# First phase of a fused RWKV, expert, attention and ternary layer: projections as three fp32r products, one activation table, joined scans, and statistics split over two engines

## The chip, the cores and the metric

One core of a Trainium2 chip runs the whole program. The metric is the device time of one execution in microseconds (us). The engines are named as in the profile: PE is TensorE (matmul), DVE is VectorE, ACT is ScalarE, POOL is GpSimd and SP is SyncE, which here only starts transfers. Each engine works through its own list of instructions strictly in the order of the code; semaphores tie the lists together.

## The reference, cut to what matters

The input x is (8, 256, 256): B = 8 sequences of T = 256 tokens with C = 256 channels. Four blocks follow each other, each with a residual and a layer norm. The change touches the first, and the routing of the second.

```python
shifted = pad(x, one token)[:, :-1]
xk = x * mix_k + shifted * (1 - mix_k)        # the same for v and r
k, v, r = xk @ Wk.T, xv @ Wv.T, xr @ Wr.T
# per channel, along the tokens, w = -exp(decay), u = first:
#   mo = max(mx, k + u);  out = (e^(mx-mo) num + e^(k+u-mo) v) / (e^(mx-mo) den + e^(k+u-mo))
#   ms = max(mx + w, k);  num, den, mx = e^(mx+w-ms) num + e^(k-ms) v, e^(mx+w-ms) den + e^(k-ms), ms
x = layernorm(x + (sigmoid(r) * out) @ Wo.T)
logits = x @ gate_w.T                         # top 2 of 8 experts, softmax of the two
x = layernorm(x + sum over the 2 of weight * expert(x))
x = layernorm(x + linear_attention(x))
x = layernorm(x + ternary_ffn(x))
```

## The kernel before

The first phase goes by sequences b = 0 to 7, in slots s. In slot s four engines work on four sequences at once: the next one's projections (s + 1), the recurrence of s, the output and residual of s - 1, and the normalised x1, the logits and the choice of experts of s - 2. Every engine has a function `a_slot(s)` whose lines are the order of its work; nothing else schedules it. Arrays of the phase are cut out of one tile called `arena`, so most rows read `arena<-arena`. A [128, 512] array is two channel halves (k = 0, 1) of 256 tokens.

- PE: `project(b, j, ...)` for j = 0, 1, 2 (k, v, r): the mix of x and the shifted x is folded into the weights `wA`, so a projection is two output halves times four products of 128 x 128 by 128 x 256 in fp32. The moving operand is `xs[b % 2]`, 257 columns per half, read from column 1 (the token) or column 0 (the one before it). Then `turn_x1` (transposes of x1), `logits`, `output` (by Wo) and `rank`.
- DVE: `exponents(s)` (a max, two scans, three subtractions), `finish_y(s - 1)`, `states(s)` (eB * v and two pairs of scans), `choose(s - 2)`, `residual(s - 1)` with `bn_stats` and `bn_aggr`, `outputs(s)` (four elementwise operations), `positions(s - 2)`.
- POOL: `deviation` turns mean and variance into the scale and bias of the norm (L1570, L1572, L1575), `weights` makes the routing weights, `scatter` sends x1 to the experts' rows in DRAM by indirect DMA.

After slot 6 the first table of expert tiles is ready, and the expert tiles begin on PE while sequence 7 ends.

Of the kernel before, what the change touches and what calls it, by code (L numbers as in the profile page):

```python
# [5 lines left out]
P = 128  # L6
# [39 lines left out]
FULL_AT = 5  # L46
FIRST = -(-(2 * FULL_AT * T - E * (P - 1)) // P)
# [27 lines left out]
def build(nc, xT, x, vecs, rows, consts, mask, Wk, Wv, Wr, Wo, gate_w, w_gate, w_up, w_down,  # L75
          Wq3, Wk3, Wv3, Wo3, W1, W2, W3, out):
    ctx = ExitStack()
    with ctx:
# [57 lines left out]
        ix8 = sb("ix8", [P, NT, 8], U32)  # L136
# [43 lines left out]
        xT_hi = sb("xT_hi", [P, KC, T], F32R)  # L180
        xT_lo = sb("xT_lo", [P, KC, T], F32R)
        x3_hi = sb("x3_hi", [P, KC, T], F32R)
        x3_lo = sb("x3_lo", [P, KC, T], F32R)
        fh = sb("fh", [P, 2, 2, T], F32R)
        fl = sb("fl", [P, 2, 2, T], F32R)

# [16 lines left out]
        def then(*shape):  # L203
            return at(place[0], shape)

        wA = at(0, (3, 2 * KC, C))
        xs = [then(KC, 1 + T) for _ in range(2)]
# [61 lines left out]
        rank_ok, row_ok, pos_ok, tanh_ok, topw_ok, scat_ok, scat2_ok = map(
            sem, ("rank_ok", "row_ok", "pos_ok", "tanh_ok", "topw_ok", "scat_ok", "scat2_ok"))  # L270
# [49 lines left out]
        def _(sp):  # L320
# [13 lines left out]
            def later(b):  # L334
# [3 lines left out]
                if b == 4:  # L338
                    sp.wait_ge(in_dnz, 1)
# [27 lines left out]
            sp.wait_ge(rp_mm, B)  # L367
# [29 lines left out]
        def _(pe):  # L397
# [15 lines left out]
            def project(b, j, dst, done):  # L413
                if j == 0:
                    pe.wait_ge(in_xsb[b % 2], 16 * (b // 2 + 1))
                if b == 0:
                    pe.wait_ge(cleared, 1)
                    pe.wait_ge(wcur_ok, j + 1)
                    pe.wait_ge(wprev_ok, j + 1)
                s = xs[b % 2]  # L420
# [1294 lines left out]
```

## Time and profile before

| | |
|---|---|
| median of 3 runs | 407.81 us (407.49 to 408.16) |
| the profiled execution, own time | 410.51 us |
| its span | 408.6 us |
| PE busy | 373.9 us, 92% |
| DVE busy | 293.4 us, 72% |
| ACT busy | 208.7 us, 51% |
| POOL busy | 129.6 us, 32% |
| first subtraction for eB, sequence 0 / sequence 7 | at 12.01 / 107.23 us |

The program's own time is a little above the span, which leaves out what lies around the first and last instruction. A row of the timeline gives start, length, engine, line, operation and operands; `x2` means two of them merged. Operations of one engine overlap a little, so what an operation costs its engine is the distance from its start to the next start (its pitch), while what waits for it waits for its end.

### The profile page before, as it was taken

The page shows a single profiled execution, that of the slowest core. Times are in us where ns is not written, and L with a number is a line of the kernel's source. Part 1 is how long each engine was busy: PE and PEld are TensorE (multiplying, and loading weights), DVE is VectorE, ACT ScalarE, POOL GpSimd, SP SyncE. Part 2 cuts the span into 40 slices and gives each one's busy share as a digit, 9 for nine tenths or more (in the row PEclk, how much of TensorE's full clock was granted, in tenths as well). Part 3 has the DMA queues.
Part 4 walks back from the last instruction along what each step waited for, and adds up shares of the span by engine and source line. Part 5 has one row for each costly group of instructions (what it writes and reads, how often), then busy time and mean ns, then how long its engine had stood idle before and what let it go on. Part 6 is the DMA issues. An engine that isn't in the chain of part 4 may idle for free.

```text
span 408.6 us, 7333 instructions
## 1 busy us (share of the span) xinstructions
PE 373.9 (92%) x2234; PEld 325.4 (80%) x2234; DVE 293.4 (72%) x774; ACT 208.7 (51%) x435; POOL 129.6 (32%) x226
## 2 busy tenths in 40 slices
PE   8999999999858999999999858999999999999781
PEld 8888888888747776777777656898999899999680
DVE  4978999999975455797453265686969687886642
ACT  5474577557745333455335322556555645645451
POOL 2002355544645500002301077435344340401111
PEclk9999999999979999999999987999999999999987
DMA  7842864301133456533431132102020200000000
GB/s 219 279 173 86 121 219 136 104 33 53 52 90 118 134 178 199 163 107 100 131 116 52 53 91 65 53 1 77 2 79 2 77 29 2 26 2 26 2 26 26
DMA packets 28565, 35.75 MB, mean 87 GB/s; under 512 B 3696, under 2 KB 25712, under 8 KB 28272
## 3 DMA queue, kind: packets, MB, share of 16 engines
q1 hardware_dynamic: 19696, 21.78, 18.0%
q0 software_dynamic: 3072, 8.39, 6.3%
q10 hardware_dynamic: 5760, 5.12, 3.6%
q8 instruction: 19, 0.31, 0.4%
q14 instruction: 18, 0.15, 0.1%
HBM read 22.83 MB, written 12.45 MB: 86 GB/s over the span
## 4 chain that ended last, share of the span: by engine, by line
PE 47%; DVE 28%; ACT 8%; issue 7%; POOL 7%; DMA 1%; SPq 0%; ACTq 0%; POOLq 0%; DVEq 0%
PE bank L400 18%; PE bank L547 10%; PE bank L568 8%; DVE st L1047 4%; POOL arena L1638 3%; POOL nm L1575 2%; PE bank L527 2%; PE bank L557 2%; PE bank L736 2%; DVE arena L1107 2%; PE bank L410 2%; DVE arena L1110 2%; POOL rs L1572 2%; DVE arena L1481 2%; ACT arena L798 1%
## 5 line engine op out<-in xcount | busy, mean ns | idle before, releaser
L400 PE MATMUL bank<-arena 128*128 128x256 f32 (+2 forms) x576 | 116.6, 357 | 1.7 <-issue 0.7
L400 PEld LDWEIGHTS bank<-arena 128*128 128x128 f32 x576 | 99.8, 190 | 14.8 <-DVE arena L1463 2.0
L798 ACT ACTIVATE arena<-bank 128x256 f32<-128x256 f32 (+1 forms) x118 | 45.5, 422 | 45.7 <-PE bank L568 30.1
L547 PE MATMUL bank<-gu,arena 128*128 x156 | 53.9, 469 | 0.0
L1570 POOL TENSOR_TENSOR ve<-mv,eps 128x2 f32<-128x2 f32 x32 | 6.8, 213 | 145.4 <-DVE mv L1051 143.6
L803 ACT ACTIVATE arena<-arena,nm,rs 128x256 f32<-128x256 f32 x48 | 26.2, 596 | 38.5 <-POOL nm L1575 38.4
L568 PE MATMUL bank<-dn,arena 96*128 x156 | 41.1, 386 | 4.6 <-DVE arena L1261 3.8
L1638 POOL DMA_INDIRECT arena<-yg,ypos x32 | 31.3, 977 | 38.9 <-DMA yg<-arena 30.5
L1261 DVE COPY arena<-bank 96x256 f32<-96x256 f32 x39 | 16.3, 419 | 36.1 <-PE bank L557 32.6
L568 PEld LDWEIGHTS bank<-dn,arena 96*128 96x128 f32 x156 | 28.6, 190 | 14.8 <-issue 6.9
L1610 POOL DMA_INDIRECT xg<-x,pos x32 | 34.3, 1073 | 14.6 <-issue 7.3
L547 PEld LDWEIGHTS bank<-gu,arena 128*128 128x128 f32 x156 | 27.1, 194 | 8.5 <-issue 0.5
L964 ACT ACTIVATE arena<-bank 128x512 f32<-128x512 f32 (+2 forms) x32 | 15.6, 488 | 25.0 <-PE bank L400 21.4
L887 ACT ACTIVATE arena<-bank 128x176 f32<-128x176 f32 x39 | 12.3, 315 | 30.8 <-PE bank L547 30.0
L400 PE MATMUL bank<-x_hi,w1q 128*128 128x256 f32 x96 | 26.5, 307 | 1.5 <-ACT x_hi L798 1.5
L1445 DVE SCALAR_TENSOR_TENSOR arena<-arena,bank 128x512 f32<-128x512 f32 (+2 forms) x32 | 17.8, 556 | 12.5 <-ACT arena L964 12.0
L681 PE MATMUL bank<-w3q,fh 128*128 128x256 f32 x96 | 24.2, 305 | 1.4 <-DVE fh L1453 0.8
L1575 POOL TENSOR_SCALAR nm<-mv,rs 128x1 f32<-128x1 f32 x64 | 24.5, 395 | 3.2
L1572 POOL TENSOR_TENSOR rs<-ve,neghalf 128x2 f32<-128x2 f32 x32 | 23.9, 748 | 2.5
L400 PE MATMUL bank<-x_lo,w1q 128*128 128x256 f32 x96 | 24.5, 287 | 0.0
L803 ACT ACTIVATE x<-x,nm,rs 128x256 f32<-128x256 f32 x16 | 8.7, 592 | 28.1 <-POOL nm L1575 28.1
L400 PE MATMUL bank<-x_lo,w2q 128*128 128x256 f32 x80 | 20.7, 288 | 0.0
(211 smaller groups left out, 864.1 us busy)
## 6 DMA issues: line engine op xcount, KB each, us to landing
arena<-xg SPq DMA_DIRECT2D x39, 128.0 KB, 2.0
yg<-arena ACTq DMA_DIRECT2D x39, 128.0 KB
arena<-in_xT SPq DMA_DIRECT2D x8, 256.0 KB
x<-in_x SPq DMA_DIRECT2D x8, 256.0 KB, 4.7
out<-arena SPq DMA_DIRECT2D x8, 256.0 KB
gu<-in_w_gate SPq DMA_DIRECT2D x1, 1408.0 KB, 7.8
gu<-in_w_up SPq DMA_DIRECT2D x1, 1408.0 KB, 7.2
dn<-in_w_down SPq DMA_DIRECT2D x11, 128.0 KB, 5.2
```

What stands on the lines that cost most here:

```text
L400: last = pe.matmul(dst, l, r, start=i == 0, stop=i == len(pairs) - 1)
L547: last = pe.matmul(bank[BANK_GU[i % 2]][:, 0:2 * F], xtT[:, i % 2, chunk(k)], w[:, :, k, :, bass.ds(e, 1), :], start=k == 0, stop=k == KC - 1)
L568: last = pe.matmul(bank[BANK_Y][:, 0:C], hT[0:HALF, i % 2, q, :], dn[0:HALF, q, bass.ds(e, 1), :], start=q == 0, stop=q == 1)
L681: last = pe.matmul(halves(7)[:, t, :], l[:, p % 2, i, chunk(t)], w3q[:, f, :], start=f == 0 and t == 0 and q == 0, stop=f == NF - 2 and q ...
L798: return act.activation(dst, src, ACT.Copy)
L803: last = act.activation(dst[:, t, :], src[:, t, :], ACT.Identity, bias=nm[:, i, t:t + 1], scale=rs[:, i, t:t + 1])
L1047: last = dve.bn_stats(st[:, i, t, :], dst[:, t, :])
L1445: dve.scalar_tensor_tensor(f, f, 1.0, times, ALU.add, ALU.mult).then_inc(fx_ok, 1)
L1572: pool.tensor_tensor(rs[:, i, :], ve[:, i, :], neghalf[:, :], ALU.pow).then_inc(dev_step, 1)
L1575: last = pool.tensor_scalar(nm[:, i, t:t + 1], mv[:, i, t, 0:1], rs[:, i, t:t + 1], -1.0, ALU.mult, ALU.mult)
L1610: pool.indirect_dma_start(out=xg, out_offset=bass.IndirectOffsetOnAxis(ap=pos[:, n, j:j + 1], axis=0), in_=x1[:, n, :], in_offset=None).th ...
L1638: pool.indirect_dma_start(out=yy[b % 2][:, t, j, :], out_offset=None, in_=source, in_offset=bass.IndirectOffsetOnAxis(ap=ypos[:, n, j:j + ...
```

## The change

Projections: x and the mixed weights are each split into a high and a low fp32r part, and each fp32 product becomes three fp32r products (high x high, high x low, low x high). The weights are split once at the start (`weights_high` on ACT, `weights_low` on DVE); x is split for each sequence, by `xs_high(b)` on ACT and `xs_low(b)` on DVE. They use tiles that later phases use.

ACT stays with one table (`natural_log_exp_and_others`): the gate is exp(-r) with a Relu in front as a floor, multiplied into the denominator, and the two routing weights come from an Exp. Each pair of scans over the two channel halves becomes one scan over 512 columns, with the decay written out in `wfull`. For sequences 0 to 5 the sum of the residual comes from an accumulating operation on DVE, and the mean and the squares are made on ACT (`spread`), with `normalise_x1` moved into the next slot. Two small casts and a subtraction leave DVE's slot. The memset of `dn` moves behind `xs_low(1)`.

```diff
             for b in range(2, B):
-                sp.wait_ge(rp_mm, b - 1)
+                sp.wait_ge(xsl_ok, b - 1)
...
             def project(b, j, dst, done):
                 if j == 0:
-                    pe.wait_ge(in_xsb[b % 2], 16 * (b // 2 + 1))
+                    pe.wait_ge(xsl_ok, b + 1)
...
-                        (wA[:, j, lag * KC + k, chunk(d)], s[:, k, 1 - lag:1 - lag + T])
-                        for k in range(KC) for lag in range(2)])
+                        pair for k in range(KC) for lag in range(2)
+                        for pair in split([w[j][:, lag * KC + k, chunk(d)] for w in (wA_hi, wA_lo)],
+                                          [s[b % 2][:, k, 1 - lag:1 - lag + T] for s in (xs_hi, xs_lo)])])
...
+            def xs_high(b):
+                act.wait_ge(in_xsb[b % 2], 16 * (b // 2 + 1))
+                past(act, rp_mm, b - 1)
+                copy(xs_hi[b % 2][:, :, 1:], xs[b % 2][:, :, 1:]).then_inc(xsh_ok, 1)
...
-                act.activation(gate[:, :, :], halves(3), ACT.Tanh, scale=0.5).then_inc(gate_ok, 1)
+                stepped(act.activation(gate[:, :, :], halves(3), ACT.Relu, bias=floor[:, :]))
+                act.activation(gate[:, :, :], gate[:, :, :], ACT.Exp, bias=floor[:, :], scale=-1.0).then_inc(gate_ok, 1)
...
+            def spread(b):
+                act.wait_ge(r_ok[0], b + 1)
+                past(act, nm_ok[0], b)
+                act.activation(mv[:, 0, :, 0], total[:, :], ACT.Copy, scale=1.0 / C)
+                stepped(act.activation(less[:, :], total[:, :], ACT.Copy, scale=-1.0 / (C * ROOT)))
+                for t in range(NT):
+                    last = act.activation(squares[:, t, :], x1[:, NT * b + t, :], ACT.Square, bias=less[:, t:t + 1],
+                                          scale=1.0 / ROOT, accum_out=mv[:, 0, t, 1:2])
+                last.then_inc(mv_ok[0], 1)
...
             def a_slot(s):
                 old, now, new = s - 2, s - 1, s + 1
                 if 0 <= old:
+                    normalise_x1(old)
+                if 0 <= s:
+                    exponents_high(s)
+                if 0 <= old:
                     copy_x1T(old)
                 if 0 <= s:
-                    exponentials(s)
+                    gate_exponentials(s)
                 keys(new)
+                if s + 2 < B:
+                    xs_high(s + 2)
                 if 0 <= old:
-                    gaps(old)
+                    odds(old)
                 if 0 <= now:
-                    normalise_x1(now)
+                    spread(now)
                 if 0 <= s:
-                    act.preload_act_table_set("natural_log_exp_and_others")
                     reciprocal(s)
...
+            def xs_low(b):
+                dve.wait_ge(xsh_ok, b + 1)
+                dve.tensor_tensor(xs_lo[b % 2][:, :, 1:], xs[b % 2][:, :, 1:], xs_hi[b % 2][:, :, 1:].bitcast(F32),
+                                  ALU.subtract).then_inc(xsl_ok, 1)
...
-                for k in range(KC):
-                    last = dve.tensor_tensor_scan(mM[:, k, :], wdec[:, k:k + 1].broadcast_to([P, T]), kP[:, k, :], LOW,
-                                                  ALU.add, ALU.max)
-                last.then_inc(wkv_step, 1)
+                dve.tensor_tensor_scan(row(mM, 0, KC * T), row(wfull, 0, KC * T), row(kP, 0, KC * T), LOW, ALU.add,
+                                       ALU.max).then_inc(wkv_step, 1)
...
+                past(dve, mv_ok[0], b)
+                for t in range(NT):
+                    last = dve.scalar_tensor_tensor(x1[:, NT * b + t, :], halves(4)[:, t, :], 1.0, x1[:, NT * b + t, :],
+                                                    ALU.mult, ALU.add, accum_out=total[:, t:t + 1])
+                last.then_inc(r_ok[0], 1)
...
                 exponents(s)
                 if 0 <= now:
                     finish_y(now)
+                if s + 2 < B:
+                    xs_low(s + 2)
                 states(s)
```

On ACT, in slot 3 before the change, from the end of `exponentials` on: eC, the gate, `keys(4)`, the routing's tanh, the norm of sequence 2, and the reciprocal. L798 is the copy out of PSUM to `kS`, L824 the pair to `kU`.

```order
54 L843 ACTIVATE arena<-arena 128x512 [waits carg_ok]
55 L846 ACT_TABLE_LOAD [waits z_ok]
56 L846 ACTIVATE arena<-bank 128x512 [waits rp_mm]
57 L798 ACTIVATE arena<-bank 128x2x256 [waits carg_ok,kp_mm]
58 L824 ACTIVATE arena<-bank,vec 128x256 x2
59 L850 ACTIVATE gap<-gap 128x2 [waits gap_ok]
60 L803 ACTIVATE x<-x,nm,rs 128x256 [waits nm0_ok]
61 L803 ACTIVATE x<-x,nm,rs 128x256
62 L873 ACT_TABLE_LOAD
63 L857 ACTIVATE arena<-arena 128x512 [waits d_ok]
64 L859 ACTIVATE arena<-arena 128x512 [waits ln_ok]
```

The same engine and slot after the change, from the exponential of eB on; row 77 (`x_hi<-arena`) is `xs_high(5)`, which signals `xsh_ok`.

```order
68 L865 ACTIVATE arena<-arena 128x2x255 [waits barg_ok]
69 L870 ACTIVATE arena<-arena,wdec 128x255 [waits aarg_ok]
70 L870 ACTIVATE arena<-arena,wdec 128x255
71 L806 ACTIVATE arena<-bank 128x512 [waits lg_ok,x1Tp_ok]
72 L875 ACTIVATE arena<-arena 128x512 [waits carg_ok]
73 L878 ACTIVATE arena<-bank,floor 128x512 [waits d_ok,rp_mm]
74 L879 ACTIVATE arena<-arena,floor 128x512 [waits act_step]
75 L806 ACTIVATE arena<-bank 128x2x256 [waits carg_ok,kp_mm]
76 L854 ACTIVATE arena<-bank,vec 128x256 x2
77 L806 ACTIVATE x_hi<-arena 128x2x256 [waits rp_mm,in_xs_odd]
78 L885 ACTIVATE gap<-mx 128x1 [waits topw_ok,route_step]
```

`xs_high` stands behind the gate and the keys, and the table loads are gone.

On DVE, in slot 3 before the change: the three subtractions, `finish_y(2)` (L1098) and the start of `states(3)`.

```order
101 L1091 TENSOR_TENSOR arena<-arena 128x2x255 [waits wkv_step]
102 L1092 TENSOR_TENSOR arena<-arena 128x2x255
103 L1093 TENSOR_TENSOR arena<-arena 128x512
104 L1098 TENSOR_TENSOR arena<-arena 128x512 [waits z_ok,inv_ok]
105 L1104 TENSOR_TENSOR arena<-arena,bank 128x2x255 [waits vp_mm,bexp_ok]
106 L1107 SCALAR_TENSOR_TENSOR arena<-arena 128x255 [waits aexp_ok]
107 L1107 SCALAR_TENSOR_TENSOR arena<-arena 128x255
```

The same place after the change (the scans are listed here as SCALAR_TENSOR_TENSOR); row 106 is `xs_low(5)`.

```order
102 L1171 TENSOR_TENSOR arena<-arena 128x2x255 [waits wkv_step]
103 L1172 TENSOR_TENSOR arena<-arena 128x2x255
104 L1173 TENSOR_TENSOR arena<-arena 128x512
105 L1178 TENSOR_TENSOR arena<-arena 128x512 [waits z_ok,inv_ok]
106 L1140 TENSOR_TENSOR x_lo<-arena,x_hi 128x2x256 [waits xsh_ok]
107 L1184 TENSOR_TENSOR arena<-arena,bank 128x2x255 [waits vp_mm,bexp_ok]
108 L1187 SCALAR_TENSOR_TENSOR arena<-arena 128x511 [waits d_ok,aexp_ok]
```

The new row waits for ACT and stands ahead of everything that `states` does.

## Rows read from the trace of the kernel before

**Rows 1.** Busy time by stretch, one slot: us, then PE, PEld, DVE, ACT, POOL

```profile
77.30:91.00 13.70, 13.70 (x73) 12.15 (x73) 13.25 (x37) 9.13 (x17) 6.85 (x10) 1.00 0.17 58
```

**Rows 2.** The chain that ended last, in order of time: start, us, what

```profile
60.74 0.20 POOL ve L1570
...
63.33 1.09 ACT x L803 x2
64.44 1.28 ACT L873
```

**Rows 3.** Timeline of DVE over slot 5: start, us, engine, line, operation

```profile
79.33 0.69 DVE L1091 TENSOR_TENSOR arena<-arena 128x510 f32<-128x510 f32 x1
...
81.16 0.68 DVE L1098 TENSOR_TENSOR arena<-arena 128x512 f32<-128x512 f32 x1
...
82.56 1.27 DVE L1107 TENSOR_TENSOR_SCAN arena<-arena 128x255 f32<-128x255 f32 x2
...
84.91 0.22 DVE L1133 MAX8 mx<-bank 128x8 f32<-128x8 f32 x2
...
86.32 0.68 DVE L1175 TENSOR_TENSOR x<-bank,x 128x512 f32<-128x512 f32 x1
...
87.99 0.66 DVE L1118 TENSOR_TENSOR arena<-arena,bank 128x512 f32<-128x512 f32 x1
...
90.49 0.18 DVE L1164 TENSOR_TENSOR hot_row<-hot,bank 128x32 f32<-128x32 f32 x1
...
91.00 0.69 DVE L1084 TENSOR_TENSOR arena<-arena 128x512 f32<-128x512 f32 x1
```

**Rows 4.** Timeline of ACT in slot 3

```profile
53.70 0.62 ACT L835 ACTIVATE arena<-arena 128x510 f32<-128x510 f32 x1
54.22 0.90 ACT L840 ACTIVATE arena<-arena,wdec 128x255 f32<-128x255 f32 x2
55.02 0.62 ACT L843 ACTIVATE arena<-arena 128x512 f32<-128x512 f32 x1
...
56.95 0.60 ACT L846 ACTIVATE arena<-bank 128x512 f32<-128x512 f32 x1
...
57.91 0.84 ACT L824 ACTIVATE arena<-bank,vec 128x256 f32<-128x256 f32 x2
```

**Rows 5.** Timeline of the start, DVE, ACT and PE

```profile
1.51 1.76 DVE L1062 MEMSET dn<- 16x2048 f32 x1 [0.39 <-issue]
...
2.71 0.20 ACT L809 ACTIVATE wdec<-vec 128x2 f32<-128x2 f32 x1 [0.16 <-DMA vec<-in_vecs]
3.62 0.91 ACT L813 ACTIVATE arena<-raw_kvr,vec 128x256 f32<-128x256 f32 x2 [0.71 <-DMA raw_kvr<-in_Wk]
...
4.79 13.41 PE L400 MATMUL bank<-arena 128*128 128x256 f32 x61
```

**Rows 6.** Timeline of DVE: first subtraction of sequences 0, 2 and 7

```profile
12.01 0.69 DVE L1091 TENSOR_TENSOR arena<-arena 128x510 f32<-128x510 f32 x1
...
37.18 0.69 DVE L1091 TENSOR_TENSOR arena<-arena 128x510 f32<-128x510 f32 x1
...
107.23 0.69 DVE L1091 TENSOR_TENSOR arena<-arena 128x510 f32<-128x510 f32 x1
```

**Rows 7.** Timeline of PE: fp32r products of the attention phase

```profile
310.87 0.28 PE L400 MATMUL bank<-kv_lo,xT_hi 128*128 128x256 f32 x1
310.99 0.27 PE L400 MATMUL bank<-kv_hi,xT_lo 128*128 128x256 f32 x1
```

**Rows 8.** Groups by line and form, later phases: busy us, mean ns | idle before

```profile
L1380 DVE SCALAR_TENSOR_TENSOR arena<-arena,topw,x 128x256 f32<-128x256 f32 x16 | 7.5, 471 | 0.2 <-issue 0.2
...
L798 ACT ACTIVATE fh<-arena 128x512 fp32r<-128x512 f32 x16 | 10.0, 627 | 4.1 <-DVE arena L1445 4.1
```

**Rows 9.** PE by stretch at the phase's end: us, PE busy, granted clock, DMA, GB/s

```profile
115.00:117.00 2.00, 0.34 (x4) 0.91 0.30 88
117.00:119.00 2.00, 1.42 (x5) 0.50 0.40 114
```

More of the change, by code:

```diff
@@ L135, in build @@
         mx8 = sb("mx8", [P, NT, 8])
-        ix8 = sb("ix8", [P, NT, 8], U32)
+        ix8 = sb("ix8", [P, NTILE, 8], U32)
+        floor = sb("floor", [P, 1])
+        negone = sb("negone", [P, NT])
+        total = sb("total", [P, NT])
+        less = sb("less", [P, NT])
         sel = sb("sel", [P, NTILE, 2])
@@ L204, in then @@
             return at(place[0], shape)
-        wA = at(0, (3, 2 * KC, C))
-        xs = [then(KC, 1 + T) for _ in range(2)]
+        wfull = at(0, (KC, T))
+        squares = then(NT, C)
+        xs = [at(3 * 2 * KC * C, (KC, 1 + T)), then(KC, 1 + T)]
         wo1 = then(KC, C)
@@ L808, in _, with weights_high, stepped @@
             act.wait_ge(in_vec, 16)
+            act.preload_act_table_set("natural_log_exp_and_others")
             act.activation(wdec[:, :], vec[:, :, TD_COL], ACT.Exp).then_inc(decay_e, 1)
-            for j in range(3):
+            act.wait_ge(unmix_ok, 1)
+            def weights_high(j):
                 act.wait_ge(in_kvr[j], 16)
                 for k in range(KC):
-                    last = act.activation(wA[:, j, k, :], raw_kvr[:, j, k, :], ACT.Copy,
-                                          scale=vec[:, k, MIX + j:MIX + j + 1])
-                last.then_inc(wcur_ok, 1)
+                    act.activation(wA_hi[j][:, k, :], raw_kvr[:, j, k, :], ACT.Copy,
+                                   scale=vec[:, k, MIX + j:MIX + j + 1])
+                    last = act.activation(wA_hi[j][:, KC + k, :], raw_kvr[:, j, k, :], ACT.Copy,
+                                          scale=unmix[:, k, j:j + 1])
+                last.then_inc(whigh_ok, 1)
+            def xs_high(b):
+                act.wait_ge(in_xsb[b % 2], 16 * (b // 2 + 1))
+                past(act, rp_mm, b - 1)
+                copy(xs_hi[b % 2][:, :, 1:], xs[b % 2][:, :, 1:]).then_inc(xsh_ok, 1)
+            steps = [0]
+            def stepped(op):
+                op.then_inc(act_step, 1)
+                steps[0] += 1
+                act.wait_ge(act_step, steps[0])
+            weights_high(0)
+            xs_high(0)
+            weights_high(1)
+            weights_high(2)
             def keys(b):
@@ L821, in keys @@
                     act.wait_ge(cleared, 1)
-                copy(kS[:, :, 1:], halves(0)).then_inc(k_ok, 1)
+                copy(kS[:, :, 1:], halves(0))
                 for k in range(KC):
@@ L917, in prepare @@
                     copy(biases[0:64, :], bias_raw[0:64, :]).then_inc(bias_hi_ok, 1)
+            normalise_x1(B - 3)
+            exponents_high(B - 1)
             copy_x1T(B - 3)
-            exponentials(B - 1)
-            gaps(B - 3)
-            act.preload_act_table_set("natural_log_exp_and_others")
+            gate_exponentials(B - 1)
+            odds(B - 3)
             turned(0)
             reciprocal(B - 1)
+            act.preload_act_table_set("silu_and_others")
             turned(1)
@@ L1105, in states @@
                 dve.wait_ge(aexp_ok, s + 1)
-                for k in range(KC):
-                    dve.tensor_tensor_scan(den[:, k, 1:T], eA[:, k, 0:T - 1], eB[:, k, 0:T - 1], 0.0, ALU.mult, ALU.add)
+                past(dve, d_ok, s)
+                dve.tensor_tensor_scan(row(den, 1, KC * T), row(eA, 0, KC * T - 1), row(eB, 0, KC * T - 1), 0.0, ALU.mult,
+                                       ALU.add)
                 dve.wait_ge(wkv_step, 4 * s + 3)
-                for k in range(KC):
-                    last = dve.tensor_tensor_scan(num[:, k, 1:T], eA[:, k, 0:T - 1], bv[:, k, 0:T - 1], 0.0, ALU.mult,
-                                                  ALU.add)
-                last.then_inc(state_ok, 1)
+                dve.tensor_tensor_scan(row(num, 1, KC * T), row(eA, 0, KC * T - 1), row(bv, 0, KC * T - 1), 0.0, ALU.mult,
+                                       ALU.add).then_inc(state_ok, 1)
             def outputs(s):
@@ L1353, in prepare @@
                 if 16 <= i < 21:
-                    for step in range(4 * (i - 16), min(19, 4 * (i - 15))):
+                    for step in range(4 * (i - 16), min(20, 4 * (i - 15))):
                         token_slots(step)
```

200 lines of the change are left out of this document (119 added, 81 removed).

## The prediction

> **What bounds the kernel now.** I first read the busy time of one slot [rows 1]. In 13.70 us PE is busy all the time and DVE for 13.25; ACT has 9.13. Two engines are full, so a gain has to come off both. Then the chain that ended last [rows 2]: through the slots it runs from DVE's statistics to POOL (60.74), to the norm on ACT at 63.33, a table load of 1.28 us at 64.44, the reciprocal and the exponentials, and back to DVE's scans. This ACT, DVE and POOL loop has the same period as the full engines. Last I read the order of work inside DVE's slot [rows 3] and ACT's [rows 4], since the change adds a hand-over between these two.
>
> **PE.** An fp32 product is two instructions of 13.41 / 61 = 0.22 us [rows 5], 0.44 us. An fp32r product has a pitch of 0.12 us [rows 7], three of them 0.36. With 24 products in a slot PE falls by 24 x 0.08 = 1.9 us, to about 11.8. PE stops being a bound.
>
> **DVE.** Pitches in the slot of before [rows 3]: max and two scans 2.03 (from the slot's start at 77.30 [rows 1] to 79.33); three subtractions 1.83; `finish_y` and eB * v 1.40 with 0.18 of waiting (82.56); four scans 2.35 (84.91); `choose` 1.41 (86.32); residual and statistics 1.67 (87.99); `outputs` 2.50 (90.49); `positions` 0.51 (91.00). Now:
> - Joined scans. Nothing shows a 512-column scan. If it costs twice a short one the gain is nothing; if each start costs some 0.06 us, three are saved in the first pair and the others together 0.18. I take 2.3 for the two later ones and 1.93 for max and scan.
> - Residual. bn_stats and bn_aggr go; two accumulating operations of 128x256 come. The nearest row is 0.47 us each [rows 8], and nothing shows the accumulator's own cost: 0.75 at the pitch of half a 512-column operation, 1.2 if each carries a small operation more. I take 1.0, 0.67 saved.
> - `choose` loses a subtraction and a cast: 1.17. `positions` loses a cast: 0.41. The four of `outputs` no longer end in a dependence: 2.4.
> - `xs_low` adds a 512-column subtraction, pitch 0.60 as the others.
>
> The sum is 1.93 + 1.83 + 0.60 + 0.60 + 0.60 + 2.3 + 1.17 + 1.0 + 2.4 + 0.41 = 12.84 us against 13.5. If that were all, a slot would fall by some 0.8 us.
>
> [...]
>
> **The new wait.** DVE's `xs_low(s + 2)` stands ahead of `states(s)`, and it needs `xs_high(s + 2)`, which on ACT stands behind `keys(s + 1)`. Let T be the start of DVE's first subtraction in slot s, whose end (T + 0.69) releases ACT. From there ACT works, by pitches [rows 4]: exp of eB 0.52 (the second exponential waits for its own subtraction, so eA starts at T + 1.32), the pair for eA 0.80, to T + 2.12; copy of x1T 0.50 as other copies out of PSUM; exp of eC 0.52; Relu 0.60 with its dependence 0.03; exp 0.52; copy to kS and pair for kU, 0.47 + 0.84; then `xs_high`, 0.63 long [rows 8]. That is T + 2.12 + 0.50 + 0.52 + 0.63 + 0.52 + 1.31 + 0.63 = T + 6.23, less about 0.1 where an independent operation starts before the end of the last: T + 6.15. DVE has done its subtractions and `finish_y` at T + 2.43. It stands still for 3.7 us. Behind that wait lie eB * v, the scans, `choose`, the residual and `outputs`, and behind them the next sequence's max, scan and subtraction, for which ACT's next slot waits. So nothing else fills the hole: it is a loop, ACT 6.15, then DVE 0.60 + 0.60 + 2.3 + 1.17 + 1.0 + 2.4 + 0.41 + 1.93 = 10.4. The period is 16.6 us in slots 2 to 5 against 13.7.
>
> Could something else in the loop be later still? PE: `keys(s + 1)` needs the k projection, and this one runs right after the r projection of the slot before, released by `seen1` in `choose`. From the rank at T - 5.5 two projections of 24 x 0.12 = 2.9 end at T + 0.4; hidden. POOL: the norm of s - 2 opens ACT's slot. Its path from the residual is `spread` (0.4 for two small operations, 1.1 for two of 128x256, a plain pair of which takes 0.91 [rows 5]), POOL 2.59 (60.74 to 63.33 [rows 2]) and the norm 1.09, 5.2 in all; the path by DVE from residual to T + 0.7 is 2.4 + 0.41 + 1.93 + 0.7 = 5.4. It is covered by 0.2 us only, so costly accumulator reads on ACT could add a few tenths per slot.
>
> **The table loads.** They leave ACT: two in a slot, 1.28 us each [rows 2], 2.6 us. Relu, `xs_high` and `spread` put 2.7 back. [...]
>
> **The start.** Before, PE began the projections at 4.79 and the weights were made by two copies per matrix from 3.62 [rows 5]. The vectors were there at 2.71 [rows 5]; now the table load of 1.28 comes after them, and the weights' copies start at 2.71 + 1.28 + 0.2 = 4.2, four of them, pitch 0.41, to 5.95; four low parts on DVE at about 0.37 to 7.45; `xs_low(0)` to 8.2. PE's k projection ends at 11.1; `keys(0)` 1.3, `xs_high(1)` 0.63, to 13.0; then DVE has `xs_low(1)` 0.65, the memset of `dn`, 1.76 [rows 5], which was hidden under the load of the weights and now lies bare, two small memsets 0.35, max and scan 1.93. So T of sequence 0 is 17.7 against 12.01 [rows 6].
>
> **The sum.** In slot 0 the wait ends at T + 5.65 (no x1T copy), then 0.6 + 0.6 + 2.3 + 2.4, the pairs' table 1.3 and 1.93: 14.8. In slot 1 the residual comes for the pairs: 14.5. Slots 0 and 1 took 37.18 - 12.01 = 25.2 us, now 29.3: +4.1. Slots 2 to 6 took 107.23 - 37.18 = 70.05 us [rows 6]; now four of 16.6 and one without `xs_low`, 12.24 + 0.5 for the first table: 79.1, +9.1. With the start's +5.7 this makes 18.9. From T of sequence 7 on the two are nearly the same: the path to the expert tiles is table, transfer, PE, and `states(7)` is reached at about the same distance. So 408.6 + 18.9 = 427.5 for the span and 410.5 + 18.9 = 429.4 for the profiled execution; the median of the runs shown lies 2.7 below that one's own time, and I forecast 427 us for it.
>
> **The rivals.**
> 1. As above, slower by the new hand-over. Chance 0.82. With scans and residual at their low prices the period is 16.2, at the high ones 16.9, with 0.3 more if the norm's path takes over; over four slots and the rest that is -3 to +4: 424 to 431.
> 2. The other side: ACT has `xs_high` ready when DVE asks, so that no hole opens. For it speaks that DVE's own work falls to 12.84 and PE's to 11.8; against it the order rows on both engines. Then slots 0 and 1 take 10.9 + 11.2, slots 2 to 5 12.84, slot 6 12.7: T of sequence 7 is 17.7 + 86.2 = 103.9, 3.3 earlier: 404.5 us. It decides by the hole's size: there are six slots with one, so the change breaks even at a hole of 3.3 / 6 = 0.55 us instead of 3.7. Chance 0.06.
> 3. [...] Chances 0.05 for the first; the second is within 1.
> 4. The shifted fp32r operand. All fp32r operands shown start at a multiple of 256 columns, these at column 1 or 257. If such a product ran at an fp32 instruction's 0.22 us, PE would need 72 x 0.22 + 3.2 = 19 us a slot and the time would be near 445. Chance 0.03.
>
> The rest, 0.04, is for what I don't see. The range, 419 to 433, takes in rival 1 with its bounds and a fall of the clock at the start. A measurement of this kernel can tell 0.2%, 0.8 us, from no change. Faster 0.07, same 0.01, slower 0.92.
>
> **What the profile would show.** `xs_low` rows on DVE with about 3.7 us idle before them, released by ACT's copy, six times; a period of 16.6 from one first subtraction to the next in slots 2 to 5 and the last at 126; PE with gaps and busy for about 12 of 16.6 us; no table load in ACT's slots; the memset of `dn` bare ahead of the first max; pitches of 0.12 in the projections. I am wrong if DVE's idle time before `xs_low` is short, if PE has no gaps, or if the later phases change by more than 1 us.

## The result and the profile after

The changed kernel takes 434.44 us (median of 4 runs, 433.26 to 434.71), the kernel before 407.8 us on the same chip: ratio 1.0647, 95% interval 1.0626 to 1.0669. It is slower, as forecast, by 26.6 us and not by 19; the time lies 1.4 us above the range. The profiled execution took 434.71 us, its span is 432.9 us.

One slot by engine, as in [rows 1] (us, then PE, PEld, DVE, ACT, POOL, the granted clock, DMA):

```profile
85.22:102.07 16.85, 14.50 (x99) 13.37 (x98) 12.51 (x31) 9.57 (x23) 8.46 (x14) 0.90 0.10 33
```

The slot is 16.85 us long instead of 13.70. No engine is full any more: DVE works 12.51 us of it, 0.7 less than before, and ACT 9.57. So something stands still that nobody covers. The timeline of DVE over slot 3 says where:

```profile
68.38 0.71 DVE L1171 TENSOR_TENSOR arena<-arena 128x510 f32<-128x510 f32 x1
...
74.95 0.69 DVE L1140 TENSOR_TENSOR x_lo<-arena,x_hi 128x512 fp32r<-128x512 f32 x1 [4.06 <-ACT x_hi L806]
...
76.16 1.21 DVE L1187 TENSOR_TENSOR_SCAN arena<-arena 128x511 f32<-128x511 f32 x1
...
78.40 0.22 DVE L1213 MAX8 mx<-bank 128x8 f32<-128x8 f32 x2
...
79.83 0.42 DVE L1261 SCALAR_TENSOR_TENSOR x<-bank,x 128x256 f32<-128x256 f32 x1
80.18 0.08 DVE L1261 DVE_READ_ACCUMULATOR x<-bank,x 128x1 f32 x1
...
80.53 0.68 DVE L1197 TENSOR_TENSOR arena<-arena,bank 128x512 f32<-128x512 f32 x1
...
82.93 0.18 DVE L1245 TENSOR_TENSOR hot_row<-hot,bank 128x32 f32<-128x32 f32 x1
...
83.25 0.68 DVE L1166 TENSOR_TENSOR arena<-arena 128x512 f32<-128x512 f32 x1
...
85.22 0.71 DVE L1171 TENSOR_TENSOR arena<-arena 128x510 f32<-128x510 f32 x1
```

The bracket at `xs_low` (L1140) is the new wait: 4.06 us for ACT's `xs_high`. Over the phase it comes six times, 3.96, 3.35, 4.78 and three times 4.06, 24.3 us in all. Set beside [rows 3], the rest is shorter or equal: two scans 2.24 (76.16 to 78.40), residual 0.70 (79.83 to 80.53), `outputs` 2.40. The same slot on ACT:

```profile
68.45 1.10 ACT L811 ACTIVATE x<-x,nm,rs 128x256 f32<-128x256 f32 x2 [0.95 <-POOL nm L1666]
69.45 0.62 ACT L865 ACTIVATE arena<-arena 128x510 f32<-128x510 f32 x1
69.97 0.90 ACT L870 ACTIVATE arena<-arena,wdec 128x255 f32<-128x255 f32 x2
70.76 0.58 ACT L806 ACTIVATE arena<-bank 128x512 f32<-128x512 f32 x1
71.24 0.62 ACT L875 ACTIVATE arena<-arena 128x512 f32<-128x512 f32 x1
71.76 0.67 ACT L878 ACTIVATE arena<-bank,floor 128x512 f32<-128x512 f32 x1
72.47 0.72 ACT L879 ACTIVATE arena<-arena,floor 128x512 f32<-128x512 f32 x1
73.09 0.58 ACT L806 ACTIVATE arena<-bank 128x512 f32<-128x512 f32 x1
73.57 0.83 ACT L854 ACTIVATE arena<-bank,vec 128x256 f32<-128x256 f32 x2
74.29 0.64 ACT L806 ACTIVATE x_hi<-arena 128x512 fp32r<-128x512 f32 x1
```

There is no table load in it, and no gap. From 69.45 to 74.93 ACT works through everything that stands ahead of `xs_high`. The first row shows what I had thought just covered: the norm waits for POOL and ends only at 69.55, so the first exponential starts 1.07 us after DVE's first subtraction and not 0.7.

At the start, PE's warm-up, the first products of the k projection, and, already in the v projection (`fh`, `fl`), the last products that ran slow:

```profile
1.38 3.86 PE L524 MATMUL bank<-ones 128*128 128x128 f32 x18 [1.38 <-DVE neghalf L1120]
8.85 0.58 PE L413 MATMUL bank<-xT_hi,kv_hi 128*128 128x256 f32 x1 [3.61 <-DVE xT_lo L1140]
9.23 0.41 PE L413 MATMUL bank<-xT_lo,kv_hi 128*128 128x256 f32 x1
9.45 0.41 PE L413 MATMUL bank<-xT_hi,kv_lo 128*128 128x256 f32 x1
...
14.78 0.38 PE L413 MATMUL bank<-xT_hi,fh 128*128 128x256 f32 x1
14.99 0.29 PE L413 MATMUL bank<-xT_lo,fh 128*128 128x256 f32 x1
15.11 0.28 PE L413 MATMUL bank<-xT_hi,fl 128*128 128x256 f32 x1
```

The pitch is 0.21 us up to 14.99 and 0.12 behind it. PE's windows there (us, busy, granted clock, DMA, GB/s) give the reason:

```profile
1.00:5.00 4.00, 3.62 (x18) 1.00 0.69 202
5.00:8.80 3.80, 0.24 (x3) 0.91 0.97 310
8.80:10.00 1.20, 1.15 (x5) 0.50 0.61 195
10.00:12.00 2.00, 2.00 (x11) 0.50 0.48 123
```

Behind an idle stretch of 3.6 us the granted clock is 0.50, and the k projection takes 5.5 us (8.85 to ACT's copy at 14.38) instead of the 2.9 that I had set.

DVE's first subtraction of each sequence, the marks of [rows 6], for the kernels of this study (us, from one profiled execution of each; e1, e3 and so on are the experiments below):

```
kernel                 b=0    b=1    b=2    b=3    b=4     b=5     b=6     b=7
before                 12.01  22.59  37.18  51.92  65.63   79.33   93.04  107.23
changed                21.47  36.43  50.78  68.38  85.22  102.07  118.91  132.53
e1  xs_low late        21.18  32.10  43.82  56.89  69.98   83.15   96.28  109.44
e2  xs_high early      21.32  32.27  43.38  56.51  69.64   82.76   95.84  109.61
e3  warm-up            18.95  33.92  48.26  65.84  83.33  100.78  118.27  132.51
e4  memset first       18.40  33.41  47.76  65.34  82.19   99.03  116.52  129.16
e6  four edits         16.31  27.25  38.16  50.85  63.81   76.93   90.01  103.18
e7  late, bn_stats     20.41  31.32  43.19  56.80  70.41   84.05   97.67  111.17
e8  late, fp32         13.34  23.65  37.43  52.84  67.66   82.48   97.30  112.72
e9  hand-over alone    12.13  30.27  46.42  66.52  85.60  104.66  123.73  137.97
e10 gaps filled        20.48  35.48  49.83  68.23  85.09  101.93  118.79  132.85
e11 start only         16.26  31.28  45.63  63.23  80.07   96.92  113.77  127.41
```

By the last mark the changed kernel is 25.3 us behind; from there to the end it takes 300.4 us and the kernel before 301.4. The whole loss lies in the first phase.

### The profile page after: what moved, and what is told of

Its sections match the earlier page's. It is cut to its first block, busy times and chain, and to the rows that moved or that the text cites. A ratio compares the mean times of both kernels' runs of the same rounds, so it can differ in the third digit from the quotient of the medians.

```text
span 432.9 us, 7770 instructions
## 1 busy us (share of the span) xinstructions
PE 376.3 (87%) x2426; PEld 333.9 (77%) x2426; DVE 293.3 (68%) x747; ACT 211.7 (49%) x484; POOL 136.7 (32%) x240
## 4 chain that ended last, share of the span: by engine, by line
PE 43%; DVE 27%; ACT 14%; issue 8%; POOL 6%; DMA 1%; ACTq 0%; DVEq 0%; POOLq 0%
PE bank L413 16%; PE bank L555 9%; PE bank L576 8%; DVE st L1102 4%; POOL nm L1666 3%; PE bank L744 2%; POOL rs L1663 2%; PE bank L689 2%; PE bank L423 2%; DVE arena L1190 2%; PE bank L565 2%; ACT arena L806 2%; PE bank L535 2%; DVE arena L1572 2%; ACT x L811 1%
## 5 line engine op out<-in xcount | busy, mean ns | idle before, releaser
L1661 POOL TENSOR_TENSOR ve<-mv,eps 128x2 f32<-128x2 f32 x32 | 7.8, 244 | 160.3 <-DVE mv L1106 107.7
L413 PE MATMUL bank<-arena 128*128 128x256 f32 (+2 forms) x192 | 39.7, 356 | 15.1 <-ACT arena L806 7.3
L413 PEld LDWEIGHTS bank<-arena 128*128 128x128 f32 x192 | 31.2, 213 | 20.7 <-ACT arena L806 8.8
L576 PEld LDWEIGHTS bank<-dn,arena 96*128 96x128 f32 x156 | 28.7, 190 | 13.1 <-issue 5.0
L413 PE MATMUL bank<-x_hi,w1q 128*128 128x256 f32 x128 | 36.4, 307 | 1.5 <-ACT x_hi L806 1.5
L1710 POOL DMA_INDIRECT xg<-x,pos x32 | 32.9, 1029 | 13.8 <-issue 7.0
L413 PE MATMUL bank<-x_lo,w1q 128*128 128x256 f32 x128 | 34.1, 290 | 0.0
L1663 POOL TENSOR_TENSOR rs<-ve,neghalf 128x2 f32<-128x2 f32 x32 | 25.9, 808 | 2.5
L413 PEld LDWEIGHTS bank<-x_hi,w1q 128*128 128x128 f32 x128 | 25.2, 197 | 1.8 <-ACT x_hi L806 1.7
L413 PEld LDWEIGHTS bank<-x_lo,w1q 128*128 128x128 f32 x128 | 25.4, 198 | 0.0
L1666 POOL TENSOR_SCALAR nm<-mv,rs 128x1 f32<-128x1 f32 x64 | 23.9, 388 | 3.2
```

What stands on the lines that cost most here:

```text
L413: last = pe.matmul(dst, l, r, start=i == 0, stop=i == len(pairs) - 1)
L576: last = pe.matmul(bank[BANK_Y][:, 0:C], hT[0:HALF, i % 2, q, :], dn[0:HALF, q, bass.ds(e, 1), :], start=q == 0, stop=q == 1)
L1663: pool.tensor_tensor(rs[:, i, :], ve[:, i, :], neghalf[:, :], ALU.pow).then_inc(dev_step, 1)
L1666: last = pool.tensor_scalar(nm[:, i, t:t + 1], mv[:, i, t, 0:1], rs[:, i, t:t + 1], -1.0, ALU.mult, ALU.mult)
L1710: pool.indirect_dma_start(out=xg, out_offset=bass.IndirectOffsetOnAxis(ap=pos[:, n, j:j + 1], axis=0), in_=x1[:, n, :], in_offset=None).th ...
```

## The experiments

The kernel before, timed beside each group of experiments, took 413.3 us for e1 to e4 (chip 9), 412.4 for e5 to e8 (chip 12), 407.9 for e9 (chip 12 too) and 408.0 for e10 to e12 (chip 4). Chip 12 stands at both ends, so the chip alone does not make the difference, and what does is not known. The changed kernel hardly follows it: 434.44 us beside 407.8, and 435.56 beside 412.4 (e5), so that its own ratio is 1.0647 in one place and 1.0543 in the other. Between groups a ratio is therefore good to about 1% only.

Where the times can't tell two kernels apart, I read the marks. They come from one execution each, and the executions of one changed kernel lie 1.5 to 7 us apart.

**e1, the wait taken out on DVE.**

```diff
                 if 0 <= now:
                     finish_y(now)
-                if s + 2 < B:
-                    xs_low(s + 2)
                 states(s)
...
                 if 0 <= old:
                     positions(old)
+                if s + 2 < B:
+                    xs_low(s + 2)
```

> The changed kernel with one edit: on VectorE the low part xs_low(s + 2) is made at the end of slot s, behind positions, and no longer ahead of states(s). Nothing else moves. Theory (the wait for ScalarE's xs_high ahead of the scans is what costs): the idle time before the six xs_low, 24.3 us in the changed kernel (3.96, 3.35, 4.78 and three of 4.06), goes, the period of slots 2 to 5 falls from 16.84 to VectorE's own 12.8, and the time is about 410 us. Rival (TensorE with its gaps and its lower granted clock is what holds the slots, and VectorE's wait only takes up slack): the period stays above 16 and the time above 428.

Measured: 412.74 us, ratio 0.9975 (0.9937 to 1.0012), against 1.0543 for the changed kernel in e5. That is no difference from the kernel before. The waits ahead of `xs_low` are all nought and the period is 13.07 to 13.17, 0.3 above DVE's own work; in slots 2 and 4 to 6, 0.20 to 0.25 of it is a wait for PE's `output`. DVE in slot 4 of e1:

```profile
76.97 0.42 DVE L1261 SCALAR_TENSOR_TENSOR x<-bank,x 128x256 f32<-128x256 f32 x1 [0.23 <-PE bank L413]
...
80.58 0.68 DVE L1140 TENSOR_TENSOR xT_lo<-arena,xT_hi 128x512 fp32r<-128x512 f32 x1
81.17 0.68 DVE L1166 TENSOR_TENSOR arena<-arena 128x512 f32<-128x512 f32 x1
81.89 1.22 DVE L1168 TENSOR_TENSOR_SCAN arena<-arena 128x512 f32<-128x512 f32 x1
83.15 0.71 DVE L1171 TENSOR_TENSOR arena<-arena 128x510 f32<-128x510 f32 x1
```

`xs_low` costs its 0.6 us of pitch and nothing else. Moving one operation wins back 23.1 us by the last mark (132.53 to 109.44). The granted clock in such a slot is 1.00 again, with PE busy for 12.4 us of 13.1: its long gaps had come from the wait.

**e2, the wait taken out on ACT.** `xs_high(s + 2)` moves ahead of the exponentials; DVE's list stays.

```diff
                 if 0 <= old:
                     normalise_x1(old)
+                if 0 <= s and s + 2 < B:
+                    xs_high(s + 2)
                 if 0 <= s:
                     exponents_high(s)
...
                 keys(new)
-                if s + 2 < B:
-                    xs_high(s + 2)
+                if s == -1:
+                    xs_high(1)
```

> The changed kernel with one edit on the other engine: on ScalarE xs_high(s + 2) is made at the top of slot s, right behind the norm and ahead of the exponentials; xs_low stays ahead of states on VectorE. Theory (the hand-over in the order of the two lists costs): VectorE finds xs_high done, its wait is under 0.5 us, but the exponentials come 0.6 us later, so the period is some 13.3 to 13.6 and the time about 412 to 414 us. Rival (xs_low ahead of the scans costs by itself, wherever its high part stands): over 425.

Measured: 412.25 us, ratio 0.9978 (0.9955 to 1.0001), period 13.1, no wait ahead of `xs_low`. The same gain as e1 from the other side: what costs is how the two lists stand to each other, and not `xs_low` ahead of the scans. That the exponentials come later by 0.6 us costs nothing; there I was 0.2 to 0.5 too high.

**e3, a longer warm-up** (`WARM = 18` instead of 9).

> The changed kernel with 18 instead of 9 matmuls on ones ahead of the first projection, so that TensorE has no idle stretch between 5.2 and 8.85 us. Theory (the granted clock of 0.50 from 8.8 to 14.8 us made the first k projection 5.3 instead of 2.9 us long, and this delay goes through to the end): 2.4 us faster, 432.0. Rival (the start is hidden behind something else): no change, 434.4.

Measured: 432.82 us, ratio 1.0461 (1.0416 to 1.0506). By the marks: 2.5 us won at the first one, as expected, and in the execution that was profiled all of it lost by the last (132.51 against 132.53). It was the slowest of the four, 434.12 us against 431.42 to 433.16, so others may have kept a part. In its slots 3 to 5 the period is 17.45 to 17.49 instead of 16.84. ACT there:

```profile
84.92 0.89 ACT L870 ACTIVATE arena<-arena,wdec 128x255 f32<-128x255 f32 x2
86.30 0.60 ACT L806 ACTIVATE arena<-bank 128x512 f32<-128x512 f32 x1 [0.49 <-PE bank L423]
```

The copy of x1T, ahead of `xs_high` in ACT's list, waits for PE's transposes. PE's windows over the projections ahead of them:

```profile
78.00:80.00 2.00, 2.00 (x13) 0.68 0.00 0
80.00:82.00 2.00, 2.00 (x12) 0.50 0.00 0
```

In the changed kernel the same two projections (80.2 to 86 us) run at 1.00, and the clock is low later, 0.52 and 0.63 in the windows from 90 to 94 us, over `output` and the v projection, for which nobody waits. Where in the slot the clock falls decides whether it costs: some 0.65 us a slot here, nothing in slots 3 to 5 of the changed kernel (e10).

**e4, the memset of `dn` at its old place.**

> The changed kernel with the memset of dn (1.76 us on VectorE) back at its old place, ahead of the first wait for the vectors. Theory (it lies bare ahead of the first max): 1.8 us faster, 432.6. Rival (hidden): no change, 434.4.

Measured: 433.89 us, ratio 1.0513 (1.046 to 1.0567). The time can't tell the theory from the rival: the interval holds e5's 1.0543, and the executions lie 3 us apart. By the marks 3.1 us are won at the first one and 3.4 at the last, and the trace shows that the memset lay bare. DVE in the changed kernel, behind the split of sequence 1:

```profile
16.26 0.69 DVE L1140 TENSOR_TENSOR x_lo<-arena,x_hi 128x512 fp32r<-128x512 f32 x1 [3.54 <-ACT x_hi L806]
17.32 1.76 DVE L1154 MEMSET dn<- 16x2048 f32 x1 [0.36 <-issue]
```

That memset with the gap ahead of it is 2.1 of the 3.07 us at the first mark. The other 1.0 is not the edit's: PE's granted clock was back at 0.85 from 12 to 14 us, where the changed kernel has 0.50, and e10 below, with nothing changed at the start, has its first mark 1.0 sooner as well (20.48; 0.80 from 12 to 14 us). How long the clock stays low at the start differs between executions.

**e5, the changed kernel again**, the reference for e6 to e8.

> [...] Ratio to the kernel before 1.055 to 1.067.

Measured: 435.56 us, ratio 1.0543 (1.0496 to 1.059), just under what I expected and well under the first run's 1.0647; it is the kernel before that was slower here. The marks are within 0.2 us of the first run's. A warning stands in its PE windows:

```profile
10.00:12.00 2.00, 2.00 (x11) 1.00 0.66 168
```

The clock reads 1.00 with 11 products in 2 us, as many as the first run has at 0.50 (e3, in the same window, 19). Its first mark is as late as the first run's, so here the count is to be believed and not the column.

**e6, a version that beats both.** e1's edit, 18 warm-up matmuls, the memset first, and:

```diff
-            act.wait_ge(in_vec, 16)
             act.preload_act_table_set("natural_log_exp_and_others")
+            act.wait_ge(in_vec, 16)
```

> The changed kernel with four edits: xs_low at the end of VectorE's slot, 18 warm-up matmuls, the memset of dn at its old place, and the table load ahead of ScalarE's wait for the vectors. Theory: the first sequence's first subtraction, at 21.18 us with the first edit alone, comes about 5 us sooner (2.4 clock, 1.8 memset, 1.3 table load, less what overlaps), the period stays 13.1, so 4.5 to 5.4 us faster than the first edit alone, ratio to before 0.985. Rival (the start's gain is given back, as the warm-up alone was, where TensorE's clock fell at another place in each slot): ratio 0.995.

Measured: 405.83 us, ratio 0.9844 (0.98 to 0.9888). The first mark is at 16.31 and the period stays at 12.7 to 13.2, so the start's gain of 4.9 us over e1 arrives whole at the last mark, and 1.4 more (103.18 against 109.44). The 1.4 comes in slots 1 to 3; in its slot 1 e1 has a granted clock of 0.56 and 0.59 from 34 to 38 us, and e6 has 1.00 all through that slot.

**e7, the statistics back on DVE**, with e1's edit; `spread` on ACT is left out.

> xs_low at the end of the slot, and the statistics of sequences 0 to 5 back on VectorE (bn_stats, bn_aggr) with the plain residual, ScalarE's spread left out. VectorE's residual goes from 0.70 to 1.67 us, so if VectorE sets the period of 13.1 it becomes 13.9 to 14.1, some 5 us more over the slots: ratio to before 1.008 to 1.01. Rival (the chain by spread, GpSimd and the norm sets the period): no slower, or faster, since that chain gets shorter by 1.4 us.

Measured: 415.27 us (median of three at 413.35 to 416.63; a fourth took 419.94), ratio 1.0114 (1.0049 to 1.0178), period 13.61 to 13.64 and not 13.9 to 14.1. The split of the statistics between DVE and ACT is worth about 0.5 us a slot, once DVE sets the pace. DVE's residual does take 1.67 us instead of 0.70, but its short waits for PE go. The rival, that the chain through ACT and POOL sets it there, falls.

**e8, the projections back in fp32**, with e1's edit and without any split of x; the low parts of the weights are left out of the computation.

> The changed kernel with the projections as single fp32 products of x and the rounded high part of the weights; the low parts of weights and x, and both splits of x, are left out, so this computes with weights of lower precision. It shows what the three fp32r products are worth, and no hand-over stands in the slots. TensorE needs 24 x 0.44 us again and sets the period: 13.7 to 13.9 against 13.1, given back in part by a start 3 us sooner without the low parts. Some 1 to 2 us above the kernel with xs_low late: ratio 1.000 to 1.003. Rival (table, scans and statistics alone bring what the change can bring): ratio 0.985 or below.

Measured: 417.89 us, ratio 1.0153 (1.0092 to 1.0213), period 14.82 and not 13.8. PE in this kernel's slot 3:

```profile
72.16 0.60 PE L423 MATMUL bank<-cst,x 128*128 128x128 f32 x4
73.45 2.89 PE L413 MATMUL bank<-arena 128*128 128x8 f32 x16 [0.69 <-ACT arena L806]
76.17 3.62 PE L413 MATMUL bank<-arena,fh 128*128 128x256 f32 x16
```

The change puts `turn_x1` behind the k projection, directly ahead of `logits`, and PE has to wait for ACT's copy in between, 0.69 us here and 0.9 us for its weight loads. With PE full this adds to its 13.7 us; I had not counted it, and it is most of the 1.1 us that are missing. So in the kernel with `xs_low` late the three fp32r products bring 14.82 - 13.1 = 1.7 us a slot. That this is near the forecast 1.9 of PE's time is chance: without the wait for the copy I estimate 0.6, from PE's 13.7 of before to the 13.1 of e1.

**e9, the hand-over alone in the kernel before.** Nobody uses the two results; the three fp32r products, the tables, the scans and the statistics are as before the change.

```diff
                 keys(new)
+                if 0 <= s and s + 2 < B:
+                    xs_high(s + 2)
...
                     finish_y(now)
+                if s + 2 < B:
+                    xs_low(s + 2)
                 states(s)
```

> The kernel before with nothing of the change but the hand-over: for sequences 2 to 7 ScalarE copies x to the fp32r tile behind keys(s + 1), and VectorE makes the low part ahead of states(s); nobody uses the two, the projections stay fp32 and the rest is as before. Theory: the loop of ScalarE (5.7 us after the first subtraction with its table load, then 0.63) and VectorE (11.7) takes 18 to 19 us in slots 2 to 5 instead of 13.7, the time is 20 to 27 us more, ratio 1.05 to 1.065. Rival (the loss comes from TensorE's changed products or the statistics on ScalarE): the two added operations cost 0.6 us a slot each at most, ratio under 1.01.

Measured: 437.49 us, ratio 1.0707 (1.0672 to 1.0741), a little above what I expected and slower than the whole change. The period is 19.07. (The edit also lets SyncE wait for `xs_low` before it loads the next x; in these slots nothing on ACT waits for that load.) DVE in slot 4:

```profile
85.60 0.69 DVE L1099 TENSOR_TENSOR arena<-arena 128x510 f32<-128x510 f32 x1
...
92.98 0.69 DVE L1110 TENSOR_TENSOR xT_lo<-arena,xT_hi 128x512 fp32r<-128x512 f32 x1 [4.88 <-ACT xT_hi L799]
...
104.66 0.69 DVE L1099 TENSOR_TENSOR arena<-arena 128x510 f32<-128x510 f32 x1
```

Two operations of 0.6 us make 5.4 us a slot: 7.38 us to `xs_low` and 11.68 behind it, one after the other.

**e10, PE's gap filled in the changed kernel**, with nine matmuls on ones ahead of `rank` in each slot.

> The changed kernel with nine matmuls on ones in each slot from 0 on, written to an unused part of bank 7, ahead of rank, where TensorE idles for 2.5 us. Theory (the loop of the hand-over sets the slots; the clock adds only 0.75 us in slot 2 and some 0.6 in slot 6, and nothing in slots 3 to 5): the clock stays at 1.00 in the slots, their period stays at 16.8 in slots 3 to 5, and 1 to 1.5 us are gained, 433. Rival (the falling clock is a large part of the loss): slots 3 to 5 get over 1 us shorter each and the time goes under 429.

Measured: 436.16 us, ratio 1.0713 (1.0674 to 1.0751), not faster but 1.7 us slower than the changed kernel beside an equal kernel before. One slot of e10, to be set beside that of the changed kernel above:

```profile
68.40:85.20 16.80, 14.83 (x115) 13.99 (x115) 12.46 (x31) 9.53 (x24) 8.37 (x12) 1.00 0.14 48
```

The clock is 1.00 and the period 16.84 to 16.86 all the same: in slots 3 to 5 the clock costs nothing. The 1 to 1.5 us that I expected in slots 2 and 6 did not come; slot 2 went from 17.60 to 18.40 and slot 6 from 13.62 to 14.06, since the nine matmuls stand in front of `rank` and delay what follows.

**e11, the start's three edits alone**, the hand-over left in.

> The changed kernel with the three edits of the start alone (warm-up, memset, table load), the hand-over left in the slots. Theory (the start costs what it costs, and the loop the rest): the first subtraction of sequence 0 comes at about 16.3 instead of 21.4, the six waits ahead of xs_low stay near 4 us, and 3 to 5 us are gained, 430 to 431, up to 2 us of it lost again where the clock falls elsewhere in a slot. Rival (hidden behind the loop): no gain.

Measured: 429.21 us, ratio 1.0508 (1.0469 to 1.0548), 5.2 us under the changed kernel (both kernels of before at 407.8 to 408.0), a little more than expected. 5.2 us at the first mark, 5.1 at the last: the start counts in full. The six waits are 3.96, 3.35, 4.78 and three of 4.06, to the hundredth those of the changed kernel.

**e12, e6 in more rounds.**

> The four edits together once more, timed in more rounds: ratio to the kernel before 0.98 to 0.99, as in the first run.

Measured: 404.17 us (12 executions), ratio 0.9913 (0.9886 to 0.9939), just above what I expected. It is faster than the kernel before both times, by 1.6% in e6 and 0.9% here, and neither interval holds 1. Between the two groups the kernel before fell by 1.1% (412.4 to 408.0) and this one by 0.4%; why is not known.

## Why the prediction was right and where it was wrong

**The mechanism** was right. `xs_low` waits six times for `xs_high`, and the wait closes a loop between ACT and DVE. Forecast 3.7 us and a period of 16.6; measured 4.06 and 16.84. e1 and e2 open the loop from its two sides and win the same; e9 closes it in the kernel before and loses as much as the whole change. That slots 2 to 5 came out near 16.6 is no luck: ACT's stretch was 0.40 us longer than the sum had it (6.55 from the mark to `xs_high`'s end), DVE's 0.13 shorter.

**What it would have been without** (rival 2): 404.5 by the sum, 3.3 us under the kernel before. e1, which is that kernel, shows no gain (0.9975, 0.9937 to 1.0012), and its last mark, 109.44, is 5.5 us later than the sum's 103.9: 3.5 from the start and 2.1 from the slots. Rival 2 was priced too low, by the same start that the forecast had too low. Only with the start repaired (e6, e12) is the time under that of before.

**The size was wrong**, and the range too narrow. The steps that failed are three terms of the sum. The largest is the start: the first subtraction of sequence 0 was set at 17.7 us and came at 21.47, most of it because the k projection, priced at 2.9 us, ran at a granted clock of 0.50 and took 5.5. Next is the step from the profiled execution to the median, 2.3 us. Third is the norm's path, called covered by 0.2 us, which set the slots: 1.7. At the last mark the sum said 18.9 us and the trace has 25.3. Term by term:

- *The start*: T of sequence 0 at 17.7, measured 21.47, +3.8. Of this about 2.5 is the clock: behind the idle stretch of 3.61 us ahead of the first projection PE's granted clock was 0.50, and where 18 warm-up matmuls fill that stretch the first mark is 2.5 sooner (e3, 18.95; that is 1.5 sooner than e10's). The forecast takes a fall of the clock at the start into its range, and the sum has no term for it. No row of the kernel before shows what such a fall costs a projection; the runs show 1.5 to 2.5 us at the first mark. Another 0.65 is the later arrival of the vectors (3.28 instead of 2.71) and the low parts' pitch of 0.40; the rest stands between `xs_low(1)` and the max.
- *Slots 0 and 1*: 29.3 forecast, 29.31 measured.
- *Slots 2 to 5*: 16.6 forecast, 17.60 and three of 16.84, +1.7. What was wrong is the norm's path, sized 5.2 us and called covered by 0.2. It took 5.8 (from the residual's end at 80.53 to the next slot's first exponential, 1.07 behind the subtraction at 85.22), and 6.2 ahead of slot 2, where that exponential came 1.8 us behind the subtraction. The term in it that was off is POOL: three operations in 3.1 us instead of 2.59, and 3.6 ahead of slot 2. By groups, in the stretch from 50 to 105 us of the changed kernel, and in the same stretch of the kernel before:

```profile
L1663 POOL TENSOR_TENSOR rs<-ve,neghalf 128x2 f32<-128x2 f32 x3 | 3.1, 1018 | 0.2
L1661 POOL TENSOR_TENSOR ve<-mv,eps 128x2 f32<-128x2 f32 x3 | 1.0, 322 | 4.8 <-ACT arena L898 4.8
```

```profile
L1572 POOL TENSOR_TENSOR rs<-ve,neghalf 128x2 f32<-128x2 f32 x4 | 2.9, 717 | 0.3
L1570 POOL TENSOR_TENSOR ve<-mv,eps 128x2 f32<-128x2 f32 x4 | 0.8, 194 | 5.8 <-DVE mv L1051 5.8
```

  The kernel before had such a case too, behind sequence 0, and the prediction did not use it; the three run to 35.89, 3.08 us in all:

```profile
32.81 0.20 POOL L1570 TENSOR_TENSOR ve<-mv,eps 128x2 f32<-128x2 f32 x1 [29.46 <-DVE mv L1051]
33.09 0.72 POOL L1572 TENSOR_TENSOR rs<-ve,neghalf 128x2 f32<-128x2 f32 x1
33.91 1.98 POOL L1575 TENSOR_SCALAR nm<-mv,rs 128x1 f32<-128x1 f32 x2
```

  In e1 the first two take 190 and 690 ns as before the change, but the pair behind them (L1666) 1.90 us instead of 1.59, 2.95 in all. So any of the three operations can be the longer one. What runs beside them may matter; that was not tried by itself, and the cause stays open.
- *Slot 6*: 12.7 forecast, 13.62 measured, +0.9, of which 0.84 is DVE's wait for `rank`, behind `output` and a v projection that began at the lower clock (0.55 and 0.60 in the windows from 124 to 128 us). e10 was meant to show that this is the clock and did not: its filler delayed the same place.
- *From the last mark on*: 1.0 us shorter than before, as forecast within 1 us.
- *The reference*: the profiled execution of the kernel before lay 2.7 us above its median, that of the changed kernel 0.3 above. I carried the sum over to the median as it stood. The spans differ by 24.3 us, the medians by 26.6; 2.3 of the 7.4 us that the forecast was off come from here. (3.8 + 1.7 + 0.9 - 1.0 + 2.3 is 7.7; the sum gave 426.7, and I wrote 427.)

**The costs by pitch**, where they could be looked up, held: two long scans 2.24 (2.3), max and scan 1.97 (1.93), `outputs` 2.40 (2.4), `xs_low` 0.60 (0.60), DVE's whole slot 12.78 (12.84). The residual was cheaper, 0.70 and not 1.0, and `choose` dearer, 1.43 and not 1.17: removing two small operations won nothing there, because the ones that stay wait for each other (0.20 and 0.21 us from start to start at 79.32 to 79.73, for operations of 0.17; before the change 0.12 at 85.58 to 85.82).

**Rival 3**, PE's clock low in every slot (chance 0.05), did happen, in part: the mean granted clock was 0.83 to 0.89 in six of the nine windows of 10 us from 40 to 130 us. It cost nothing in slots 3 to 5 of the changed kernel (e10), and 0.65 us a slot in e3, where it lay over the projections that ACT waits for. By an estimate from the pitches at the start, 0.21 us at 0.50 and 0.12 at 1.00, two whole projections (48 products) at 0.50 would take 4.3 us longer; no slot shows that.

**Rival 4** falls: the shifted fp32r products have the pitch of the others, 0.12 us.

**The accumulators.** In the changed kernel each accumulating operation of DVE's residual has a read of its own behind it, 0.08 us long (80.18 in the timeline of slot 3). It costs nothing there: the next operation starts with it, and the two operations have a pitch of 0.35 us each. ACT has such reads too, in `spread`: 0.19 us long with a pitch of 0.09 (81.39 to 81.48).

## What to carry to other kernels

Where an in-order engine is given a step that needs another engine's result of the same slot, write down what stands ahead of both and go once round the loop: the period is the sum of the two stretches, however little either engine is busy (here 16.85 us with DVE busy for 12.51 and ACT for 9.57). If nobody needs the result in that slot, put the step at the end of the slot; here one moved line is worth 23 us, over 5% (132.53 against 109.44 at the last mark, ratios 1.0543 and 0.9975). When a path is covered by only 0.2 us, treat it as a second bound with a cost of its own. If the sum has an idle stretch ahead of a matmul that everything waits for, price that matmul at a lower clock too (here 0.50 behind 3.61 us, 2.5 us at the first mark), and put it into the range together with the other terms. And make the sum against the profiled execution, but ask how far that lies from the median before carrying it over.

## What the runs showed of the hardware

- In the changed kernel PE's granted clock was 0.50 from 8.8 us on behind 3.6 us without work, though the engine had been busy for 3.62 of the 4 us from 1 to 5, and rose after 14 us (0.76 from 14 to 16, 1.00 behind it); with 18 warm-up matmuls instead of 9 (e3) PE did 19 products in each 2 us from 10 us on, at 1.00. By the pitch of 0.21 instead of 0.12 us the low stretch at the start was 3.4 us long in e4 and e10 (9.45 to 12.84 in e10) and 6.1 in the changed kernel (8.85 to 14.99). In two profiles the clock column reads 1.00 from 10 to 12 us with 11 products (e1 and e5): the number of products in a window is the surer witness.
- In slots 2 to 5 of e3 and of the changed kernel, with gaps of 1 to 2.6 us, the clock was low in a part of each slot (down to 0.50 or 0.52 in windows of 2 us), and in which part differed from kernel to kernel: over the projections of e3, over the v projection of the changed kernel.
- One scan over 512 columns has a pitch of 1.11 to 1.13 us, two over 256 take 1.16 to 1.19: joining saves some 0.06 us a pair.
- The same three POOL operations of the norm (L1570, L1572 and L1575, after the change L1661, L1663 and L1666) took 2.6 to 3.6 us, and 2.6 or 3.1 within one execution of the kernel before.
- The kernel before took 407.8 to 413.3 us by group of runs, 1.3% apart, with every execution of a group within 0.6% of its median; chip 12 had 412.4 once and 407.9 once. The changed kernel moved by 0.3% between two such groups.
